# Another order of three TensorE products in the second side group of a transformer-block kernel

## The reference, cut to what matters

```
h = layernorm(x) * (1 + ca) + sa
qkv = h @ Wqkv.T + bqkv; q, k, v per head
attn = softmax(q @ k.T / sqrt(8)) @ v
x1 = x + ga * (attn @ Wo.T + bo)
h2 = layernorm(x1) * (1 + cb) + sb
probs = softmax(h2 @ router_w.T); top 2 -> weights
out = x1 + gb * sum over the two of (h2 @ expert_e.T + prob_e) * weight_e
```

## Time and profile before

| | |
|---|---|
| median of 3 runs | 552.03 us (551.75 to 552.13) |
| the profiled execution | 553.11 us |
| its span, first to last instruction | 551.3 us |
| TensorE busy (matmul) | 521.9 us, 95% |
| ScalarE busy | 494.8 us, 90% |
| VectorE busy | 362.3 us, 66% |
| GpSimd busy | 218.5 us, 40% |
| mean granted TensorE clock | 0.993 |

### The profile page before, as it was taken

The page is one execution under the profiler, slowest core; times in us unless marked ns, Lnnn a source line. Parts: engine busy times, 40 slices in busy tenths (PEclk is TensorE's granted clock), DMA queues, the critical chain, the costliest instruction groups (busy, mean ns, idle before and its releaser), DMA issues. The chain is left out here.

```text
span 551.3 us, 14315 instructions
## 1 busy us (share of the span) xinstructions
PE 521.9 (95%) x4092; PEld 219.7 (40%) x4092; DVE 362.3 (66%) x1269; ACT 494.8 (90%) x571; POOL 218.5 (40%) x429
## 2 busy tenths in 40 slices
PE   8789899999999999999999999999999999999982
PEld 7633334343434343434343434343434343433251
DVE  4445467666786766667767666667676666664466
ACT  1489999999999999999999999999999999999952
POOL 1223333344444334444443344444433444443335
PEclk9999999999999999999999999999999999999997
DMA  4563333333233333333323333333233333332010
GB/s 110 157 182 89 95 85 94 101 99 86 70 85 82 87 99 99 98 87 76 79 79 89 98 99 98 87 79 76 79 89 97 99 98 86 89 72 79 17 32 15
DMA packets 83953, 48.44 MB, mean 88 GB/s; under 512 B 59964, under 2 KB 74696, under 8 KB 83912
## 3 DMA queue, kind: packets, MB, share of 16 engines
q1 hardware_dynamic: 68842, 43.33, 29.2%
q10 hardware_dynamic: 15070, 4.56, 4.5%
HBM read 32.91 MB, written 14.94 MB: 87 GB/s over the span
## 5 line engine op out<-in xcount | busy, mean ns | idle before, releaser
L545 ACT ACTIVATE probs<-ps_scores 128x1024 f32<-128x1024 f32 x512 | 485.8, 1029 | 38.0 <-PE ps_scores L713 29.0
L731 PE MATMUL ps_attn<-probs,values 128*32 128x512 f32 x2048 | 247.3, 601 | 0.0
L713 PE MATMUL ps_scores<-query_stack,key_stack 32*128 32x512 f32 x1024 | 130.8, 500 | 15.5 <-ACT probs L545 9.4
L713 PEld LDWEIGHTS ps_scores<-query_stack,key_stack 32*128 32x128 f32 x1024 | 49.4, 183 | 166.4 <-ACT probs L545 162.1
L419 POOL TENSOR_SCALAR var_eps<-moments 128x1 f32<-128x1 f32 x64 | 12.2, 190 | 220.8 <-DVE moments L1080 148.4
L731 PEld LDWEIGHTS ps_attn<-probs,values 128*32 128x32 f32 x2048 | 53.8, 109 | 109.2 <-issue 109.0
L761 PE MATMUL ps_side<-experts_gated,h2T 128*128 (+1 forms) x228 | 74.7, 410 | 0.0
L1069 DVE RECIPROCAL sums_inv<-sums 128x128 f32<-128x128 f32 x32 | 30.4, 951 | 31.3 <-DMA attnT<-a_scr 31.3
L1076 DVE TENSOR_TENSOR x<-ps_side,x_gated 128x128 f32<-128x128 f32 x31 | 9.0, 291 | 62.1 <-PE ps_side L761 58.7
L1152 DVE TENSOR_TENSOR weighted<-ps_side,coef 128x256 f32<-128x256 f32 x114 | 46.5, 408 | 2.4 <-PE ps_side L761 2.4
L468 POOL TENSOR_TENSOR mix<-weighted 128x512 f32<-128x512 f32 x31 | 39.6, 1278 | 0.0
(11 more groups left out here) (130 smaller groups left out, 510.0 us busy)
## 6 DMA issues: line engine op xcount, KB each, us to landing
key_stack<-k_scr SPq DMA_DIRECT2D x128, 128.0 KB, 2.8
query_stack<-q_scr SPq DMA_DIRECT2D x125, 64.0 KB, 2.2
q_scr<-qk_parts SPq DMA_DIRECT2D x94, 64.0 KB, 1.7
k_scr<-qk_parts SPq DMA_DIRECT2D x64, 64.0 KB, 1.7
a_scr<-attn ACTq DMA_DIRECT2D x126, 18.0 KB
sums<-a_scr SPq DMA_DIRECT2D x32, 64.0 KB, 2.1
attnT<-a_scr SPq DMA_DIRECT2D x32, 64.0 KB, 2.3
out_dram<-out_all ACTq DMA_DIRECT2D x29, 64.0 KB, 1.7
```

The lines of the kernel that those rows point to most:

```text
L545: nc.scalar.activation(probs[:, k % RING, g, :], ps_scores[:, slot(k, g), :], ACT.Exp, scale=SCALE)\
L713: mm = nc.tensor.matmul(out_, key_stack[p0:p0 + 32, parity, 2 * k:2 * k + 2, :].rearrange("p j r -> p (j r)"), query_stack[p0:p0 + 32, par ...
L731: mm = nc.tensor.matmul(ps_attn[q:q + 32, :], values[:, parity, g, k, :], probs[:, k % RING, g, h * HALF:(h + 1) * HALF], start=(k == 0), ...
```

## The change

In side1, TensorE issues the expert product first, then the transpose, then the value products. VectorE's reading of the group waits for the value products, and in tile 31, which has none, for the transpose. It then weighs the expert piece before it makes `h2T`. In tile 31, TensorE's wait ahead of side2 is for `h2T`. Nothing is computed otherwise than before.

```diff
             def side1(ps, at, batch, parity, before, after, past):
 
+                if past < 4 <= before:
+                    c_experts(ps, at[-4], batch[4], parity, 3)
                 if past < 2 <= before:
                     c_transpose(ps, at[-1])
                 if before >= 2 and after >= 1:
                     a_project_v(ps_side[:, P:2 * P], at[2], 1 - parity)
-                if past < 4 <= before:
-                    c_experts(ps, at[-4], batch[4], parity, 3)
 
             def drained1(at, before, after, past):
 
                 if before >= 2 and after >= 1:
                     reached(pe, ev["values_done"], at[2])
-                elif past < 4 <= before:
-                    reached(pe, weighted_done[3], at[-3])
                 elif past < 2 <= before:
                     reached(pe, ev["h2T_done"], at[-1])
...
             def written1(at, before, after, past):
 
-                if past < 4 <= before:
-                    reached(dve, experts_done[3], at[-3])
-                elif before >= 2 and after >= 1:
+                if before >= 2 and after >= 1:
                     reached(dve, ev["v_ps_done"], at[2])
+                elif past < 2 <= before:
+                    reached(dve, ev["x1hatT_done"], at[-1])
...
+                if past < 4 <= before:
+                    c_weigh(banks[1], at[-3], parity, 3)
                 if past < 2 <= before:
                     c_h2T(banks[1], at[-2], at[-1], parity)
-                if past < 4 <= before:
-                    c_weigh(banks[1], at[-3], parity, 3)
```

## The result

The changed kernel takes 549.85 us in the median of 17 runs (549.31 to 552.76), the kernel before in the same rounds 553.29 us (551.75 to 554.83). The ratio is 0.9948, 95% interval 0.9936 to 0.9959: 2.9 us less (2.3 to 3.5). The profiled execution spans 548.1 us against 551.3, at a granted clock of 0.984 against 0.993, so the clock doesn't explain the shorter span. The same changed kernel once more, beside another kernel in five rounds, gave 0.9938 (0.9918 to 0.9957).

The account below looks back on a forecast made before the run. TensorE was taken as late in side1, 1.71 us against ScalarE's floor of 1.62. Net 0.082 x 27 = 2.2 us, so 552.03 - 2.2 = 549.8 us; 80% range 549.0 to 551.1, forecast's chance 0.82.

Parts of the forecast that it names:

- The floor of 1.62 and what side1 had above it: Scores 2 to 3: exchange with ScalarE sets 1.62 us; side1 lies about 0.087 us above it in 27 tiles.
- The pieces in the new order: TensorE's side1: scores to experts 0.44, experts 0.53, transpose 0.21 to 0.26, values 0.38; 1.56 to 1.61 us against 1.71.
- Values before scores, the unpriced neighbour, 0.38: End of side1: value products directly before scores 3, not priced by the trace, taken as 0.38 us.
- Rival 1: Side1: value products before scores are dear; no gain at 0.48 us, 555.3 us in all at 0.60; chance 0.04.
- Rival 2, order is worth nothing: Side1's four pieces are additive, 1.71 us again in any order, so 552.0 us; chance 0.09.
- The waits for `x1hat` and `values`: TensorE's transpose and side2: neither wait appears; margins 0.54 us for `x1hat`, 0.36 for `values` less 0.087.
- neither reaches TensorE: VectorE's 0.20 us of issue before `h2T` may be hidden or paid twice; no effect on TensorE either way.
- other work of its own: GpSimd before its mix at 269.90: busy otherwise, so a weighed piece 0.33 us earlier gains nothing.
- Rival 3, "the gain is taken elsewhere": TensorE less off the floor, or `values` last before side2; near 551 to 552 us; chance 0.05.
- The size: Whole kernel: 0.087 us gained a tile, some 5 ns given back, net 0.082 x 27 = 2.2 us.
- ScalarE's wait at step 4: ScalarE's idle time at step 4 of a tile falls from 0.22 to about 0.14 us.
- Two of the signs: Timelines: scores 3 noted as waiting for ScalarE; ScalarE's total of waits for scores down some 2 us.

Follow-up runs that it names:

- e4: Changed kernel with expert piece 3 issued twice (experts, experts, transpose, values); executed once, scores 2 to 3 in 1.989 us.
- e3: Kernel before with expert piece 3 issued twice (transpose, values, experts, experts); executed once, scores 2 to 3 in 2.139 us.
- e1: Changed kernel with VectorE's old reading order, so only TensorE's new order against the kernel before; ratio 0.9997 (0.9987 to 1.0008).
- e8: Changed kernel with side1 as transpose, experts, experts, values (piece 3 issued twice); executed once, scores 2 to 3 in 1.943 us (median).
- e10: The changed kernel unaltered, run once more beside another kernel; ratio to the kernel before 0.9938 (0.9918 to 0.9957), median 550.19 us.
- e6: Changed kernel with side1 as experts, experts, values, transpose (piece 3 issued twice); executed once, scores 2 to 3 in 2.139 us.

## Why the prediction was right, and where only its sum was

- **The floor of 1.62 and what side1 had above it**: right. All 27 distances are 1.618 to 1.620 after the change.
- **The pieces in the new order**: right. 0.44, 0.54 to the transpose, 0.20 to the values. TensorE alone needs 1.56 us by e4, at the lower end of 1.56 to 1.61, so the transpose's load is hidden. The sentence of the Trainium skill (TensorE: Matmul & The Clock Gate, "What overlaps and what doesn't") by which a weight load overlaps running matmuls only in other row groups does not hold for these full-width loads: in e4 the second to fourth expert pass start 0.215 us apart, each with its load of 0.19 us behind the pass before.
- **Values before scores, the unpriced neighbour, 0.38**: right by e4. Rival 1 falls: it is far from the 0.48 where the gain would end.
- **Rival 2, order is worth nothing**: falls; e3 and e4 differ by 0.15 us on TensorE.
- **The waits for `x1hat` and `values`**: right, neither appears.
- **VectorE: "neither reaches TensorE"**: wrong. The step followed `values` and the weighed piece from the moved instructions and stopped there. It also took the time before GpSimd's mix for "other work of its own", while GpSimd had stood idle for `pair_w` there (1.86 us in tile 16, 64.9 us in its 31 waits). It did not follow what is queued behind them: `pair_w`, GpSimd's coefficients, mix and squares, and the norm product in side3. That wait was already what came last in side3, by the 0.016 us above the floor. The whole chain keeps its distance from scores 2, so a shorter side1 brings scores 6 forward and leaves the squares where they were; e1 shows the loss in every tile of the loop. The hidden 0.20 us of issue, which the prediction mentioned and priced at nothing, is what keeps the gain: `pair_w` comes 0.25 us earlier, of which that wait is 0.20. Rival 3, "the gain is taken elsewhere", was the right shape at the wrong place, and with TensorE's part alone it would have come true.
- **The size**: 2.2 us forecast, 2.2 us in the distances of the trace, 2.9 (2.3 to 3.5) by the ratio, whose interval begins just above the forecast. That it fits so well owes something to two omissions of opposite sign: side3 gave 0.4 us that were not expected, and the other distances took back 0.5 instead of 0.13. The ratio's rest is not explained by an instruction; start-up and the single stall, together 1.0 us between these two traces, are of that size and differ from trace to trace. The time forecast, 549.8 us, meets the measured 549.85 in part by luck: it was a step of 2.2 from 552.03, and in the rounds of the comparison the kernel before took 553.29.
- **ScalarE's wait at step 4**: 0.22 us before, and after the change too short for the timeline to note; 0.14 from the start times, as forecast.
- **Two of the signs**: a wait noted at scores 3, as in the earlier trace rows, did not appear, though ScalarE is last there by 0.05 us. The total of ScalarE's noted waits for scores in the loop fell from 11.8 us to 2.5, not by "some 2 us", because waits of 0.14 us are no longer listed at all. Taken from the start times, ScalarE's idle stretches in tiles 4 to 30 add up to 15.7 us before and 13.0 after, 0.5 of the difference being the stall in tile 5. That leaves the 2 us forecast.

```profile
ACT probs L545 <- PE ps_scores L713: 2.5, 6, 0.8
```

## What to carry to other kernels

On an engine whose array is used now whole, now in slices, put products of one division next to each other: here one change less and a hidden weight load saved 0.15 us together, or 0.20 where the longer load was the one hidden. Then stop at the floor that the partner engine sets; what is saved beyond it is only reserve. And before counting a shorter stage as a gain, look at every wait later in the same cycle whose releaser is tied to a point ahead of the shortened stage: in relation to that wait it comes later by just what was saved, and where the margin is zero, the gain is lost there.

## What the runs showed of the hardware that was not expected

- Full-width fp32 passes with a 128-column weight load each follow one another every 0.215 us at 256 columns; the load of 0.19 us is fully behind the pass before, on the same rows. The first pass after another division of the array costs 0.32 (e4, and the finish).
- The length of side1 on TensorE can be added up to some 10 ns from the prices of neighbours (1.989 and 1.943 measured in e4 and e8, 1.98 to 2.00 and 1.94 to 1.95 expected).
- VectorE's address work for an operand with a register index (0.10 and 0.05 us on its queue, 24 times, for `h2T`) goes with 0.20 us of standstill where it stands behind a 0.15 us instruction, and with some 0.02 us behind one of 0.42 us. In the written-out tiles, where `h2T` has no such rows, there is no standstill behind `pair_eps` either:

```profile
L1090 DVEq FUSED_REGOPS  x24: 99/99/110, 92.8 to 453.0; - x24
L1090 DVEq ALU_OP  x24: 45/45/45, 93.0 to 453.1; - x24
```

- In nine of the twelve traces one distance in tile 5 or 28, the second tile of the loop and the first behind it, is 0.2 to 0.9 us too long (e10 has one of 0.08, e8 two of 0.1, in tiles 4 and 5, e6 none); its place and size change from trace to trace. What causes it stays open.
